# TensorE fills its gaps between the stages with products of constants into a bank that nobody reads

## What is computed

```python
x = x + _L0_conv_ref(_gn(x), Wq, bq, Wk, bk)      # attention over 4096 pixels
x = x + _L1_conv_ref(_gn(x), w1, in_gamma, in_beta, w2, b2)   # involution: 3x3 weights per pixel
x = x + _L2_conv_ref(_gn(x), dw_w, dw_b, ln_g, ln_b, w1, b1, w2, b2, ls)   # 7x7 depthwise, norm, MLP
x = x + _L3_conv_ref(_gn(x), offset_w, offset_b, weight, ...)  # deformable 3x3 convolution
```

## Time and profile before

| | us |
|---|---|
| median of 3 runs | 4148.88 (4147.64 to 4153.2) |
| the profiled execution | 4145.01 |
| its span | 4143.2 |
| mean granted clock in it | 0.905 |
| TensorE busy | 3416.2 (82%) |
| VectorE busy | 3239.3 (78%) |
| GpSimd busy | 2234.6 (54%) |
| ScalarE busy | 1972.0 (48%) |

### The profile page before, as it was taken

How to read it: one execution, slowest core, us unless ns; L and a number is a source line. 1 busy time by engine, 2 the same in 40 slices (tenths; PEclk the granted TensorE clock), 3 DMA queues, 4 the chain that set the end, 5 groups by cost and what they waited for, 6 DMA issues and landing times.

```text
span 4143.2 us, 79222 instructions
## 1 busy us (share of the span) xinstructions
PE 3416.2 (82%) x28785; PEld 2163.6 (52%) x28785; DVE 3239.3 (78%) x6687; ACT 1972.0 (48%) x4413; POOL 2234.6 (54%) x2476
## 2 busy tenths in 40 slices
PE   4999868879999966979999976979999976982555
PEld 2666623447777732336777742435777752342444
DVE  5999767489999856669999956749999966745666
ACT  2444332446666622346666742345666653242333
POOL 3454450068878641038878824018887845005775
PEclk9999989989999988979999988989999998995555
DMA  1000101155555402055555512045555520117775
GB/s 49 9 12 12 42 7 44 60 165 148 154 151 156 120 19 49 14 160 154 150 151 151 153 40 48 2 127 143 156 152 152 151 80 22 39 46 213 219 220 176
DMA packets 219934, 426.57 MB, mean 103 GB/s; under 512 B 27825, under 2 KB 126540, under 8 KB 217512
## 3 DMA queue, kind: packets, MB, share of 16 engines
q0 software_dynamic: 92160, 302.06, 25.3%
q1 hardware_dynamic: 127346, 119.53, 10.0%
q10 hardware_dynamic: 54, 0.01, 0.0%
HBM read 340.77 MB, written 60.65 MB: 97 GB/s over the span
## 4 chain that ended last, share of the span: by engine, by line
PE 37%; DVE 29%; issue 12%; POOL 10%; POOLq 4%; DVEq 3%; ACT 2%; SPq 2%; DMA 1%; ACTq 0%
DVE val L1233 9%; PE bank L548 7%; DVE mxc L1196 7%; PE bank L688 6%; DVE xl L1256 5%; POOL G L1595 3%; DVE val L1243 3%; PE bank L732 3%; PE bank L716 2%; POOLq L1570 2%; PE bank L749 2%; PE bank L475 2%; POOL reg L1595 1%; POOL x_cur L1595 1%; PE bank L571 1%
## 5 line engine op out<-in xcount | busy, mean ns | idle before, releaser
L1606 POOL TENSOR_TENSOR xl<-pt 128x192 bf16<-128x192 f32 (+1 forms) x1024 | 685.5, 670 | 422.6 <-PE bank L548 206.4
L868 ACT ACTIVATE pt<-bank 128x512 f32<-128x512 f32 x1024 | 608.2, 594 | 573.9 <-PE bank L517 343.0
L1595 POOL DMA_INDIRECT G<-patch_table,idx x576 | 593.9, 1031 | 191.9 <-issue 115.1
L548 PEld LDWEIGHTS bank<-vt,pt 128*128 128x128 bf16 x8192 | 548.5, 98 | 242.1 <-ACT pt L868 3.9
L548 PE MATMUL bank<-vt,pt 128*128 128x129 bf16 (+1 forms) x8192 | 632.7, 220 | 1.1 <-ACT osb L876 1.1
L1196 DVE TENSOR_REDUCE mxc<-bank 128x1 f32<-128x512 f32 x896 | 607.1, 679 | 29.0 <-PE bank L475 27.3
L1256 DVE TENSOR_TENSOR xl<-pt 128x320 bf16<-128x320 f32 (+1 forms) x1024 | 504.2, 493 | 72.8 <-PE bank L548 53.7
L548 PE MATMUL bank<-vt,xl 128*128 128x129 bf16 x4096 | 401.2, 221 | 12.8 <-DVE xl L1256 12.7
L1580 POOL TENSOR_TENSOR rs<-ve,mhalf 128x4 f32<-128x4 f32 x32 | 34.9, 1092 | 619.6 <-ACT ve L995 619.6
L475 PE MATMUL bank<-reg,qh 128*128 128x512 bf16 x896 | 341.4, 382 | 13.6 <-DVE mxc L1196 10.1
L688 PE MATMUL bank<-reg,val 128*32 128x512 bf16 x3264 | 271.4, 395 | 66.4 <-DMA G<-xl 66.4
(11 more groups left out here) (249 smaller groups left out, 6906.2 us busy)
## 6 DMA issues: line engine op xcount, KB each, us to landing
patch_table<-valt SPq DMA_DIRECT2D x64, 512.0 KB, 6.6
G<-patch_table,idx POOLq DMA_INDIRECT x576
x_cur<-in_x SPq DMA_DIRECT2D x4, 2048.0 KB, 8.1
xl<-in_x SPq DMA_DIRECT2D x32, 256.0 KB
attn_out<-ob SPq DMA_DIRECT2D x32, 256.0 KB
x_store<-x_cur SPq DMA_DIRECT2D x4, 2048.0 KB, 6.5
xr<-x_store SPq DMA_DIRECT2D x32, 256.0 KB
out<-fo SPq DMA_DIRECT2D x32, 256.0 KB
```

Source lines behind the costliest of these rows:

```text
L548: last = mm(O[t // 2][:, c0:c0 + width], image[:, at % ring, t * 128:(t + 1) * 128], vhl[:, values, st, 0:width], start=(st == 0 and part ...
L868: A(pt[:, at % PT_RING, :], ST[at % ST_RING] if n else ST_FIRST[at % 3], ACT.Exp, scale=SCALE).then_inc(s["exp_done"], 1)
L1595: g.indirect_dma_start(out=patches(j, k), out_offset=None, in_=table[:], in_offset=bass.IndirectOffsetOnAxis(ap=idx[:, j * K1 + k:j * K1 + ...
L1606: g.tensor_tensor(pl[:, at % PL_RING, 0:stop], pt[:, at % PT_RING, 0:stop], ph[:, at % PT_RING, 0:stop], ALU.subtract).then_inc(s["pl_p"], 1)
```

## The change

A helper, `keep_busy(bank, count)`, issues `count` products on TensorE: the identity `identb` as weights, four of the nine blocks of `l1w2_s` as the moving operand (128x512, bf16), the result into a PSUM bank that no one reads afterwards before it is overwritten. The products wait for nothing and signal nothing. It is called at eleven places; what stands around them is as before, and the work of all other engines too.

```diff
+            def keep_busy(bank, count):
+                for _ in range(count):
+                    mm(P[bank], identb[:], l1w2_s[:, 0:CH // C, :], start=True, stop=True)
...
                     mm(ST[c % 2][:], l1w1_s[:], rows(c), start=True, stop=True).then_inc(s["t_ps"], 1)
+                keep_busy(5, 20)
                 wait_alone(pe, s["tl_rdy"], NCH * n + 1)
...
                     if conv:
                         taps(12, 22)
+                    elif norm:
+                        keep_busy(2, 7)
                     if norm:
                         pe.wait_ge(s["ln_sq"], B)
...
                     if conv:
                         taps(25, PE_TAPS).then_inc(s["dwp"], 1)
+                    elif norm:
+                        keep_busy(2, 3)
...
             def sample(n, dcn):
+                if dcn:
+                    keep_busy(2, 18)
                 group_norm(4 * n)
+                if dcn:
+                    keep_busy(2, 8)
                 attention(n, dcn)
+                keep_busy(5, 50)
                 group_norm(4 * n + 1)
+                keep_busy(5, 18)
                 layer1(n)
+                keep_busy(5, 6)
                 group_norm(4 * n + 2)
+                keep_busy(5, 55)
                 layer2(n)
+                keep_busy(5, 6)
                 group_norm(4 * n + 3)
+                keep_busy(5, 28)
                 layer3_prepare(n)
```

## The result

| | before | after |
|---|---|---|
| median, us | 4148.88 (4145.4 to 4153.2, 5 runs) | 4126.62 (4122.84 to 4130.41, 5 runs) |
| the profiled execution | 4145.01 | 4124.26 |
| its span | 4143.2 | 4122.5 |
| mean granted clock | 0.905 | 0.935 |

The account below looks back on a forecast made before the run. TensorE's clock falls to half while it waits at changes of stage, slowing each next stage's first work. Terms 8.4 + 0.3 + 2.8 + 6.2 + 6.0 + 1.7 = 25.4 us off 4145.0, plus 3.9 for the median: 4123 us, range 4105 to 4139.

Parts of the forecast that it names:

- the case that was called the likeliest: The forecast itself: 4113 to 4132 us, chance 0.54, with layer 2's first taps mostly still starting at the low clock.
- The t products: Before layer 1's taps: 18 added products let them start at the high clock, mean 2.1 us per sample, 8.4 in all.
- even: The 18 before layer 1 taken to end level with the wait for ACT; bounds 1.9 us early, 1.9 late.
- The 20 before layer 1's taps: After the t products: first taps run high but DVE is still busy; 0.3 us in all, bound 1.2 per sample.
- Layer 2's start: 6 and 55 products around GroupNorm before layer 2's taps: 0.7 us per sample, 2.8 in all, bounds 0 and 4.2 per sample.
- the first rival: Layer 2 starts high as well, if the 55 end within about 2 us of the taps: 4110 us; chance 0.18.
- The last norm step: Layer 2, 7 and 3 products: L716 group takes 3.67 us, 1.55 saved each, 6.2 in all; lower bound a third.
- a wait of 1.4 us is enough: In layer 2's last norm step, such a wait drops the clock: one L716 group takes 5.32 us against 3.67.
- The convolution: Before layer 3, 6 and 28 products: starts high, 1.9 us saved, 0.4 late; net 1.5 per sample, 6.0 in all.
- GroupNorm and the samples' starts: 18 and 8 at starts of samples 1 to 3: GroupNorm saves 0.2 to 0.4 us; with 0.2 after attention, 1.7 in all.
- the products don't lift the clock: Everywhere: identity weights, almost all zeros, count for nothing, so runs end late; 60 us slower, 4209; chance 0.05.
- Much of it is eaten: Norm step low by chance, the 28 and 18 late, layer 2 gives nothing: 4136 us, 4141 or more if worse; chance 0.20.

## Why the prediction was right, step by step

The predicted 4123 lies 3.6 below the measured 4126.6. That closeness is partly luck, since before's median was 4145.8 to 4147.5 in the later rounds, where it was 4148.9 here. But the case that was called the likeliest happened: the t products, the norm step and the convolution run at the high clock from their start, and layer 2 does not. Term by term, with the means of two profiles of each kernel:

- *The t products: 8.4, measured 8.6.* They take 7.4 to 7.5 us, the figure given. The 18 ended 0.27 us ahead of them in sample 1, and in the other samples of that profile the t products followed without a wait, so "even" was a fair choice between early and late.
- *The 20 before layer 1's taps: 0.3, measured nothing.* DVE sets that stage, as the step said.
- *Layer 2's start: 2.8, measured 0.3* (1.1 gained up to the first variance product, 0.5 lost behind it, 0.3 ahead of the taps, of which sample 3's late image is the most). The mechanism is as described. The 6 run low and the 55 behind them high, these end 3.4 us early in sample 1 (3.5 was said), and the clock falls as the taps begin. The size was too large even so, and the upper bound, 4.2 a sample, was far too large. The step halved the low stretches as if all of that were on the path, and put the second DMA wait in half a sentence. The kernel without the 6 shows what stands in its place: at a high start the taps wait for the image's second part up to 3.9 us. Its profile gains 1.1 us up to the first variance product and loses more behind it, so it shows nothing of the first rival's 13 us more, though the rival's condition can be had. (The 4105 given there "if the 28 are never late" does not follow either: by the prediction's own 0.4 a sample it is 4110 less 1.6.)
- *The last norm step: 6.2, measured 6.8.* The group takes 3.68 us in place of 5.1 to 5.4. The lower bound was no idle worry: in two samples of the kernel with only the 6 and 28, the group was fast with nothing added in the step. The same samples show that the reading "a wait of 1.4 us is enough" was too simple, since that wait stands ahead of groups of 3.67 and of 5.38 alike. The step keeps its gain in after, where the gaps behind it are filled too; with the 7 and 3 alone 5.5 of the 6.8 us were lost behind it.
- *The convolution: 6.0, measured 5.2.* Gained 7.4, where four times 1.9 were said; lost 2.2, where four times 0.4 were said. The mean lateness is about right, but it comes as 2.0 in one sample and up to 0.4 in another. In sample 2 the clock was low for 5.8 us and more of the run, which the step's formula prices at 6.0 + 2.9 us against a wait of 7.1.
- *GroupNorm and the samples' starts: 1.7, measured about 0.3* (0.6 gained on the way into attention, 0.3 lost ahead of the t products, both within what two executions differ by). GroupNorm's two products do save the 0.40 us at each start. The step counted it as if the chain behind kept it; the kernel with these groups alone shows it lost, in two of three samples, to products that run low behind the wait for Pool. In after the query projection ran low in samples 1 and 2 (2.01 and 2.07 us), and there 0.4 was left behind that wait.

So 21.1 of 25.4 was there. The missing 4.3 are 2.5 at layer 2's start, 1.4 at the samples' starts, and smaller differences. Both large ones are one slip: a gain at one product was counted as time, although what came behind it (a wait for a DMA, or products at the low clock) could take it back.

Of the rivals, "the products don't lift the clock" is ruled out by the rise in the run of 55 that began low (two stretches of the kernel without the 6, sample 1), with identity weights and nothing else on TensorE:

```profile
1570.90:1576.00 5.10, 5.10 (x12) 1.81 (x12) 1.44 (x2) 4.17 (x4) 0.55 (x1) 0.50 0.07 17
1576.00:1585.00 9.00, 8.95 (x42) 4.04 (x41) 8.11 (x12) 5.04 (x5) 0.00 (x0) 1.00 0.56 134
```

"Much of it is eaten" happened in part, at the 28 alone. The pace of the added products was 0.215 us in every run, and 0.43 where the clock was low, as taken from the earlier trace rows.

## What to carry to other kernels

Filling a wait of TensorE with products that nobody reads pays where TensorE's own first work sets the next stage, and here it had to last nearly to the end of the wait: where it ended 3.4 us ahead of layer 2's taps, the clock fell as the stage began; where it ended 0.7 to 1.8 us ahead, the stage began at 1.00; where it ended too late, every 0.215 us was lost. Size each filling for both levels of the clock, and price the gain by what the stage waits for next. Without the 6 the taps got to their second part 1.8 us sooner, by the mean of four samples, than in before's two profiles, and waited 2.0 us longer for it. A stage that no edit touches (attention's values, 5.3 us between two executions of the same kernel) can hide an effect of this size in single profiles, so stages are compared over two of each.

## What the runs showed of the hardware beyond that

Where the low stretch of one place was missing, the next one was longer. With only the norm step filled, the next convolution stayed low for longer (0.84 against 0.99 in its second stretch) and the convolution stages took 2.9 us more than in the first profile of before; where the step was fast with nothing added, the convolution behind it was longer by 0.5 too. And the same place can be high or low between samples of one execution with the same instructions around it (3.67 and 5.38 us for one group). Single edits of this kind are therefore not quite additive, and a place that shows a low clock in one profile need not show it in the next.
